# A graph layer and a routed expert layer on one core: the last tiles' list entries by one-hot products, the expert weights loaded in another order

## The reference

```python
x = x + gnn(layernorm(x), edges)                 # segment softmax over the edges of each row, then elu
x = x + ffn(layernorm(x))

def ffn(x):
    gate_logits = x @ gate_w + gate_b            # 16 experts
    topk_vals, topk_idx = jax.lax.top_k(gate_logits, 2)
    topk_w = jax.nn.softmax(topk_vals, axis=-1)
    h = jax.nn.relu(jnp.einsum('bsh,ehf->bsef', x, w1) + b1)        # 256 -> 512
    expert_out = jnp.einsum('bsef,efh->bseh', h, w2) + b2           # 512 -> 256
    y = x + jnp.sum(topk_w[..., None] * expert_out[topk_idx], axis=2)
    return layernorm(y) * gamma + beta
```

## Time and profile before

| | |
|---|---|
| time, median of 3 runs | 2786.66 us (2780.65 to 2787.5) |
| the profiled execution's own time | 2785.81 us |
| its span, first to last instruction | 2783.8 us |
| busy: PE, DVE, ACT, POOL | 1707.9, 1755.6, 1125.4, 1863.6 us |
| mean granted TensorE clock | 0.815 of full |
| HBM read and written | 355.94 and 36.52 MB |

### The profile page before, as it was taken

One profiled execution on the slowest core, in us unless ns is written; L12 is line 12 of the kernel. 1 busy time (PEld: TensorE's weight loads), 2 busy tenths in 40 slices (PEclk: granted clock), 3 DMA queues, 4 the chain that ended last, 5 costly groups with the idle time before them and its releaser, 6 DMA issues. The chain is left out here.

```text
span 2783.8 us, 44516 instructions
## 1 busy us (share of the span) xinstructions
PE 1707.9 (61%) x8882; PEld 1388.8 (50%) x8883; DVE 1755.6 (63%) x4256; ACT 1125.4 (40%) x2079; POOL 1863.6 (67%) x1938
## 2 busy tenths in 40 slices
PE   6445656556555556555566565655655638999970
PEld 5334444444444444444444444444444427999970
DVE  7655666666666566666666666666666636565557
ACT  3424344343443443443434434434344323443433
POOL 2267777777777777777777777777777624555543
PEclk9768877888888787788787787877877869999995
DMA  6445555555555555555555555555555355333346
GB/s 210 108 130 147 132 146 145 136 145 133 147 146 132 145 149 132 146 137 143 145 133 145 149 131 147 146 134 145 135 145 146 97 187 169 105 105 101 106 121 246
DMA packets 206790, 393.03 MB, mean 141 GB/s; under 512 B 73265, under 2 KB 129338, under 8 KB 200484
## 3 DMA queue, kind: packets, MB, share of 16 engines
q0 software_dynamic: 90992, 262.35, 36.9%
q1 hardware_dynamic: 93144, 109.62, 13.1%
q10 hardware_dynamic: 22620, 20.70, 2.6%
HBM read 355.94 MB, written 36.52 MB: 141 GB/s over the span
## 5 line engine op out<-in xcount | busy, mean ns | idle before, releaser
L1269 POOL DMA_INDIRECT gat<-table,idx x1627 | 1544.7, 949 | 505.4 <-issue 482.5
L1367 PE MATMUL ps_sum<-msg,hot 128*128 128x264 f32 x3322 | 1069.3, 492 | 778.8 <-DVE msg L1414 670.0
L1367 PEld LDWEIGHTS ps_sum<-msg,hot 128*128 128x128 f32 x3322 | 811.0, 250 | 985.1 <-issue 802.5
L1414 DVE TENSOR_TENSOR msg<-gat,ps_weight 128x2304 f32<-128x2304 f32 x196 | 471.6, 2406 | 31.1 <-ACT ps_weight L1324 27.3
L1324 ACT ACTIVATE ps_weight<-score 128x72 f32<-128x72 f32 x196 | 45.0, 230 | 591.1 <-DVE score L1405 590.9
L1411 DVE TENSOR_TENSOR hot<-ps_own,rel 128x1152 f32<-128x1152 f32 x196 | 250.3, 1277 | 0.0
L1403 DVE TENSOR_TENSOR both<-gat,ps_own 128x144 f32<-128x144 f32 x196 | 58.0, 296 | 288.0 <-DMA gat<-table,idx 286.7
L2116 PE MATMUL ps_ht<-xT,w_t 128*128 128x128 f32 x1712 | 214.7, 280 | 14.7 <-DVE w_t L2148 14.7
L2043 POOL DMA_INDIRECT chosen<-o_sb,put_at x105 | 115.6, 1101 | 148.2 <-DMA chosen<-o_sb,put_at 96.0
L2116 PEld LDWEIGHTS ps_ht<-xT,w_t 128*128 128x128 f32 x1712 | 205.4, 197 | 14.9 <-DVE w_t L2148 14.9
L2125 PE MATMUL ps_o<-w_sb,hidT 128*128 x840 | 200.0, 381 | 0.0
(11 more groups left out here) (397 smaller groups left out, 2124.5 us busy)
## 6 DMA issues: line engine op xcount, KB each, us to landing
dst_row<-dst_half SPq DMA_DIRECT2D x49, 1088.0 KB
gat<-table,idx POOLq DMA_INDIRECT x1661
b_t<-in_L_ffn_b_dram ACTq DMA_DIRECT2D x107, 128.0 KB, 3.0
w_sb<-in_L_ffn_w_dram SPq DMA_DIRECT2D x6, 2048.0 KB, 19.3
listing<-list_f SPq DMA_DIRECT2D x736, 0.5 KB
table<-rows SPq DMA_DIRECT2D x49, 128.0 KB, 1.7
y_rows<-y SPq DMA_DIRECT2D x49, 128.0 KB, 3.3
x_all<-in_x_dram SPq DMA_DIRECT2D x6, 896.0 KB, 8.9
```

Source lines behind the costliest of these rows:

```text
L1269: pool.indirect_dma_start(gat[:, GSTART[g] + k, :], None, table, bass.IndirectOffsetOnAxis(ap=idx[g][:, k:k + 1], axis=0)).then_inc(landed ...
L1367: made = pe.matmul(ps_sum[:, 0:SUM], hot[:, m, k, :], msg[:, m, k, :], start=(g == 0 and k == 0), stop=(g == NG - 1 and k == n - 1))
L1414: dve.tensor_tensor(msg[:, m, 0:n, 0:D].rearrange("p j (h d) -> p j h d", d=HD), gat[:, j:j + n, 0:D].rearrange("p j (h d) -> p j h d", d=HD),
```

## The change

- `settle` no longer computes addresses. For tiles 47 and 48 it keeps, for each expert, the place in its list (`late_place`); only tile 46 is scattered (two indirect writes in place of six), and the fetch of the lists waits for these two alone (`put` 32).
- The entries of tiles 47 and 48 come in by four products of one-hot matrices on PE (`late_row`, `late_lane`), accumulated in the bank where the fetched lists are transposed. DVE builds them while the fetch is under way.
- `y` of the last tile goes to another buffer (`xn`), and does not wait for the store of tile 47's.
- SP stores tile 47's `y` ahead of the first weights. The first load has three experts; the loads are 0-2, 3-4, 5-7, 8-11, 12-15. In the expert loop SP has at most two loads under way, and signals each one when it has landed, counting single experts.
- Four gathers of rows are issued ahead of the expert loop, in place of three.
- DVE's first 16 steps are written out (8 before). In steps 1 and on of these, gate and `minus_y` come before the copy of w1. The additions to `x_all` stand in steps 8 to 14.
- Four constants that POOL made with iota are derived by DVE from others.

```diff
-WLOADS = ((0, 2), (2, 4), (4, 8), (8, 12), (12, 16))
+DVE_HEAD = 4
+BETA_AT = 8
+WLOADS = ((0, 3), (3, 5), (5, 8), (8, 12), (12, 16))
...
-    def settle(self, dve, link, a, n, ps_route):
-        link(dve.tensor_tensor(self.base_f[:, :], self.base[:, :], self.expert_row[:, :], ALU.add))
+    def settle(self, dve, link, a, ps_route, place):
         dve.wait_ge(self.ranks_done, a + 1)
-        link(dve.tensor_tensor(self.base_f[:, :], self.base_f[:, :], ps_route[:, EXPERTS:2 * EXPERTS], ALU.add))
-        dve.tensor_tensor(self.base[:, :], self.base[:, :], ps_route[:, 2 * EXPERTS:3 * EXPERTS], ALU.add)
-        link(dve.tensor_tensor(self.hit[:, :, :], self.base_f[:, :].unsqueeze(1).to_broadcast([P, 2, EXPERTS]),
-                               self.pick[:, :, :], ALU.mult))
-        link(dve.tensor_reduce(self.at_f[:, :], self.hit[:, :, :], AX.X, ALU.add))
-        dve.tensor_copy(self.at_i[:, n, :], self.at_f[:, :]).then_inc(self.spots_ready, 1)
+        dve.tensor_tensor(place, self.base[:, :], ps_route[:, EXPERTS:2 * EXPERTS], ALU.add)
+        link(dve.tensor_tensor(self.base[:, :], self.base[:, :], ps_route[:, 2 * EXPERTS:3 * EXPERTS], ALU.add))
...
         @block.gpsimd
         def _(pool):
-            pool.iota(tile_of[:, :], pattern=[[0, 1]], base=0, channel_multiplier=1,
-                      allow_small_or_imprecise_dtypes=True).then_inc(consts, 1)
...
             pool.wait_ge(finish.listed, 16 * EXPERTS * (a - 1))
-            for n in range(3):
-                finish.scatter(pool, a - 1 + n, n)
+            finish.scatter(pool, a - 1)
             pool.wait_ge(steps, 1)
-            pool.wait_ge(finish.put, 96)
+            pool.wait_ge(finish.put, 32)
...
-            pool.wait_ge(steps, 4)
+            pool.wait_ge(steps, 5)
             pool.sem_inc(pool_turn, 1)
-            for i in range(FFN_AHEAD):
+            for i in range(FFN_BODY):
...
+            for c in range(4):
+                pe.matmul(ps_ids[:, 0:P], late_lane[:, c, :], late_row[:, c, :], start=(c == 0), stop=False)
+            pe.wait_ge(steps, 4)
+            pe.matmul(ps_ids[:, 0:P], ids_f[:, :], ident[:, :], start=False, stop=True).then_inc(turned, 1)
...
             sp.wait_ge(w_in[0], 32)
-            sp.sem_inc(w_ready, 1)
-            for k in range(FFN_AHEAD):
+            sp.sem_inc(w_ready, WLOADS[0][1])
+            for k in range(B):
                 sp.wait_ge(x_in[k], 16)
+            load_weights(sp, 1, w1, w2, w1_sb, w2_sb, w_in)
             for q in range(1, len(WLOADS)):
-                load_weights(sp, q, w1, w2, w1_sb, w2_sb, w_in)
-            for q in range(1, len(WLOADS)):
-                sp.wait_ge(w_in[q], 32)
-                sp.sem_inc(w_ready, (WLOADS[q][1] - WLOADS[q][0]) // 2)
+                if q + 1 < len(WLOADS):
+                    load_weights(sp, q + 1, w1, w2, w1_sb, w2_sb, w_in)
+                sp.wait_ge(w_in[q % 2], 32 * (q // 2 + 1))
+                sp.sem_inc(w_ready, WLOADS[q][1] - WLOADS[q][0])
...
-                if head and 1 <= i <= NGRP:
-                    if i == 1:
+                if head and 0 <= i - BETA_AT < NGRP:
+                    if i == BETA_AT:
                         dve.wait_ge(scale_in, 16)
```

More of the change, by code:

```diff
@@ L136, in build @@
         norms = Norms(sem)
-        w_in = [sem(f"w_in{q}") for q in range(len(WLOADS))]
+        w_in = [sem(f"w_in{q}") for q in range(2)]
         weights, listers, nodes = (ctx.enter_context(ExitStack()) for _ in range(3))
@@ L1706, in lower, with norm_outer @@
         act.activation(self.low[:, :], self.low[:, :], ACT.Exp).then_inc(self.exp_ready, 1)
-    def norm_outer(self, act, a):
+    def norm_outer(self, act, a, y=None):
         act.wait_ge(self.scale2_ready, a + 1)
-        if not (isinstance(a, int) and a == 0):
+        if y is None and not (isinstance(a, int) and a == 0):
             act.wait_ge(self.sent, a * 16)
-        act.activation(self.y[:, :], self.x(a), ACT.Identity, bias=self.nmr[:, bass.ds(a, 1)],
+        act.activation((self.y if y is None else y)[:, :], self.x(a), ACT.Identity, bias=self.nmr[:, bass.ds(a, 1)],
                        scale=self.rstd[:, bass.ds(a, 1)]).then_inc(self.y_ready, 1)
@@ L1935, in _ @@
             finish.weigh(dve, link, a, b)
+            dve.tensor_reduce(owner[:, :], mine[:, 1:X1], AX.X, ALU.add)
+            dve.scalar_tensor_tensor(held[:, :], tile_of[:, :].to_broadcast([P, 2]), -float(P), found[:, 1:3], ALU.mult, ALU.add)
+            link(dve.scalar_tensor_tensor(late_place[:, :, :], begin[:, 0:EXPERTS].unsqueeze(1).to_broadcast([P, 2, EXPERTS]), float(P),
+                                          late_place[:, :, :], ALU.mult, ALU.add))
+            dve.tensor_scalar(owner[:, :], owner[:, :], float(EXPERTS - 1), None, ALU.min).then_inc(steps, 1)
@@ new lines, in _ @@
+            dve.tensor_tensor(late_lane[:, :, :], late_lane[:, :, :],
+                              finish.ids[:, a:b + 1, :].rearrange("p t c -> p (t c)").unsqueeze(2).to_broadcast([P, 4, P]),
+                              ALU.mult).then_inc(steps, 1)
+            dve.wait_ge(ids_in, 16)
+            link(dve.scalar_tensor_tensor(ids_f[:, :], lane[:, :], held[:, 1:2], ids_f[:, :], ALU.is_lt, ALU.mult))
+            dve.tensor_tensor(ids_f[:, :], ids_f[:, :], rest[:, :], ALU.add).then_inc(steps, 1)
@@ L1936, in _ @@
+            dve.wait_ge(turned, 3)
+            link(dve.tensor_copy(put_all[:, :], ps_ids[:, 0:P]))
+            dve.tensor_scalar(get_all[:, :], put_all[:, :], 1, None, ALU.arith_shift_right).then_inc(steps, 1)
+            dve.wait_ge(steps, 5)
+            link(dve.scalar_tensor_tensor(second[:, :], get_all[:, :], -2.0, put_all[:, :], ALU.mult, ALU.add))
+            dve.tensor_copy(expert_l[0:1, 4:L + 4], ps_ids[0:1, P:2 * P])
             link(dve.tensor_scalar(passes_f[:, :], begin[:, EXPERTS:X1], float(FFN_LAG + FFN_BODY - 1), None, ALU.add))
@@ L2146, in first_weight, with weigh @@
                 e = expert(dve, i - back, -back)
-                dve.wait_ge(w_ready, (e >> 1) + 1)
+                dve.wait_ge(w_ready, e + 1)
                 dve.tensor_copy(w1_t[:, k % 2, :, :], one4(w1_sb[:, bass.ds(e, 1), :, :])).then_inc(w1_ready, 1)
+            def weigh(o, i, b):
+                dve.wait_ge(x_tr, i)
+                if not (isinstance(i, int) and i < 3):
+                    dve.wait_ge(o_ready, i - 2)
+                dve.scalar_tensor_tensor(gate[:, b:b + 1], xt[:, b, D + 1:YROW], second[:, bass.ds(i - 1, 1)], xt[:, b, D:D + 1],
+                                         ALU.mult, ALU.add)
+                dve.scalar_tensor_tensor(minus_y[:, o, :], xt[:, b, 0:D], second[:, bass.ds(i - 1, 1)], xt[:, b, 0:D],
+                                         ALU.mult, ALU.subtract).then_inc(gate_ready, 1)
             def step(k, i, head):
```

170 lines of the change are left out of this document (86 added, 84 removed).

## The result

| | before | changed |
|---|---|---|
| time, median, in the same session | 2785.76 us (2780.65 to 2787.5) | 2770.32 us (2768.5 to 2772.0) |
| the profiled execution's own time | 2785.81 us | 2769.94 us |
| its span | 2783.8 us | 2768.1 us |

The forecast was 2765 us, and the time lies in its range. 15.4 of the expected 21 us came. The ratios of the experiments leave out two executions, of 3595 and 6669 us, that ran at a lower granted clock than those beside them.

The account below looks back on a forecast made before the run. Bounds: a serial chain in the last tiles, DVE's wait for SP at loop start, then PE. First product -9.8 us; with the loop's deliveries tile 12 is -20.3, taken as -21: 2764.8, shown as 2765 us, range 2750 to 2776.

Parts of the forecast that it names:

- Last `y` in its own buffer, shorter `settle`: Last tiles: no wait for the earlier tile's store, -3.9 us; fewer small operations and no scatter for 47 and 48, -1.2.
- Lists without the last scatters: Last tiles: list fetch no longer waits for the last scatters; with the two parts before, gather -10.3 us, first product -9.8.
- The 3 MB load: First weight load, larger and later: landed by 2244, needed at 2255, so it costs nothing, with cover of 11 us.
- Signals load by load: Start of expert loop: DVE's 23.68 us wait for SP goes, and no copy waits again.
- What a tile costs beside a load: Expert loop while weights load: 6.66 us a delivery, from a single row, with bounds 3.76 and 8.3.
- x_all in steps 8 to 14: Expert loop: DVE's additions bound those steps at 4.51 us against 3.76; those beside the load are covered.
- behind tile 12 both programs are bound by PE: Rest of the expert loop: PE sets the pace in both programs, so the gain taken at tile 12, -21 us, stays.
- Stage 7: POOL's "ISA" instruction moves here: at 7.8 us it costs nothing, and idle time takes up to about 18 us.
- A: Expert loop: tiles lose nothing beside the load; tile 12 at about 2318, -36, 2750 us; chance 0.16.
- B: Expert loop: tiles lose more, 8.3 us a delivery; with dear one-hots 2774 us; chance 0.15 together with the late-signal rival.
- C: Expert loop: first copy waits if the 3 MB land after 2255; 2770 us at 2260; chance 0.15 with the dearer-tiles rival.
- D: Stage 7: moved instruction takes over 18 us and delays the additions; at 45 us, 2792 us; chance 0.03.

Follow-up runs that it names:

- the second profile: The changed kernel run and profiled once more, on a chip with 2791.93 us for the kernel before: 2773.89 us, ratio 0.9943.
- the run with the load ahead: The changed kernel with the first 3 MB load sent ahead of the store of tile 47's rows: 2774.68 us, ratio 0.9947.
- The run with the iota kept: The changed kernel with one POOL iota, whose result nobody reads, at the start of the last tiles: 2771.71 us.
- last tiles alone: The changed kernel with the old `stage6`, `load_weights` and `WLOADS`: ratio 0.9955.
- the old loads: The changed kernel with the old `WLOADS` (experts 0-1, 2-3, 4-7, 8-11, 12-15), signals still load by load: ratio 0.9947.
- without loads: The changed kernel with no weights issued in the expert loop, tiles from 4 on using expert 2's (another result): tile 40 at 170.3 us after the first product.
- the runs from step 3: The changed kernel with the `x_all` additions in steps 3 to 9: ratio 0.9951; the same with the first load ahead of tile 47's rows: 2766.63 us, ratio 0.9923.

## Why the prediction was right, and where it was off

The sum was -21 us. The traces have -16.2 from the mark to tile 40 (-16.0 in the second profile), and the medians -15.4 and -18.0. The gains came by the mechanisms told. What was missed is an overlap on PE, the landings beside the first load, and the end of the loop's slow part; each took from the gain.

- **Last `y` in its own buffer, shorter `settle`: right.** `xn_f` starts 0.04 us after its scale is written, and `row_i` comes 5.7 us sooner behind the mark (-5.1 forecast).
- **Lists without the last scatters: right in kind; the first product gained 7.5 us (8.8 in the second profile) where 9.8 was taken.** Behind the mark (2228.1 before), the forecast put the end of the one-hots at 20.9 us, the first gather at 23.6, the product at 28.9. The one-hots ended at 19.8, 1.1 sooner. Then the step that failed: "PE's product (0.5; its four others run meanwhile)". They read the last one-hot, so they run behind it, not meanwhile. In the run with the load ahead, where the lists were early, the gather left 4.1 us after the one-hots in place of the 2.7 reckoned: **1.4 us**. The products take 2.08 us at a granted clock of 0.50 (the lower level, 1.2 GHz), and part of that lies beside DVE's operations on `ids_f`. From gather to product it was 6.0 us where 5.3 was reckoned: 0.7.
- **The 3 MB load, "Nothing: cover of 11 us": right for its reader, wrong for its neighbours.** It was reckoned landed by 2244, at the full rate from its first byte, and landed at 2251.2; from 2239 to 2247 the core moved only 178 GB/s. Sending it ahead of tile 47's rows did not cure that (140 GB/s from 2243 to 2247). The run with the iota kept, in which they left later and the fall came later, points at tile 46's scatters of 4-byte elements; no run leaves them out, so the cause isn't shown. Nobody waited for the weights, but the fetch beside them took 5.0 us in place of 2.5, and the second scatter, reckoned landed, held it back by 0.6. That is the other 1.4 us of the first profile (0.2 in the second, with a landing of 4.5 and no wait for the scatter).
- **Signals load by load: right.** Without it 23.52 us are still waited (last tiles alone); with it none, or 3.30 with the old loads.
- **What a tile costs beside a load, 6.66 us: right,** though from a single row, and that it held so closely is in part luck. It was 6.73, and 3.93 without loads, where PE sets the pace. The Trainium skill ("DMA: Bandwidth & Descriptors", on arbitration) has each DMA engine take turns between queues, a packet at a time. The estimate drawn from that rule, that a delivery is held up by its own length, 0.4 us, isn't borne out here: the landing took 5.8 us beside the load and 3.5 without it.
- **x_all in steps 8 to 14: right in price; the end of its reach was missed.** Seven additions in the quiet cost 3.6 to 6.4 us over the same seven beside the loads (the runs from step 3), about the 7 x (4.53 - 3.76) that the step reckons with (its own row gives 4.51, not 4.53).
- **The loop at tile 40: 7.2 to 8.7 us in place of 11.2,** the larger part of the miss. From the first product to tile 12 the forecast has 76.9 us, and the profiles have 77.2 and 79.9: nearly nothing missed in the first, 3.0 us in the second. Then the step "behind tile 12 both programs are bound by PE": from tile 12 to tile 40 it was 104.6 us before and 106.1 and 105.0 in the changed kernel, 1.5 and 0.4 lost, and tiles 12 to 13 and 13 to 14 are still 4.85 and 4.19 us apart in the first profile. The last 0.7 is that -21 was taken where the deliveries gave -20.3. What the 3.0 us of the second profile are stays open.
- POOL's indirect writes beside an addition take longer: 2.35 us for tile 8's in the changed kernel, 2.70 without loads, 0.99 elsewhere. The Trainium skill ("SBUF — State Buffer", the rules on the shared port pair) has a DVE operation with two inputs in SBUF lock out a GpSimd operation that reads SBUF. The longer rows agree with that, though not every write beside an addition is long, and no run shows that it is the ports. Forecast to be free, it may be some of what the loop lacks; no run separates it.
- **Stage 7: right in what it costs.** The moved instruction takes up to 10.1 us there (from 2690.48, when the stage begins, to 2700.54), and beyond 9 us it moves the first addition, by 1.2 to 1.6 us. The end of the stage does not move.
- **The rivals.** A is out (6.73 us, not 3.8), B too (its own 8.3 us), C did not occur in this order, though its mechanism, a 3 MB load that is slower than its rate, is what stood beside the late lists; D's instruction stayed far from 18 us.
- **The signs.** Three of the prediction's own signs went against it, though the time came as forecast. DVE's second operation did wait for the fetch (2.38 us). The first product came at 2261.25, after the 2261 named as wrong; but the mark stood 1.9 us later in this execution, and behind it the product came at 31.2 us, where the limit was 32.9 and the forecast 28.9. And the first addition of stage 7 came 10.1 us into the stage, past the 9 us of rival D, of whose mechanism that much is there, at no cost. The 380 GB/s that are put down to the earlier trace rows aren't in them (355); single stretches of 4 us in the trace before have 380.

## What to carry to other kernels

A load that is early enough for its own reader may still be late for its neighbours: small transfers beside it land at twice their time, and in an order where a store stands behind it, the load's size comes straight into the chain (11.1 us in place of 4.3). Changes of loads and of what runs beside them should be tried together: with the old order of stores the third expert cost the loop's change 6 us, with the new it gained 2. An operand that is built in parts joins the chain with its last part, and so do all products of it. A small scattered write beside a bulk load may be dearer than it looks: here the load's rate fell from 391 to 132 GB/s behind two of them, which are a likely cause and not a shown one. Bulk loads that delay a serial chain of small landings were cheaper in a row than spread (one experiment, this loop), and other engines' extra work was cheapest beside them.

## What the runs showed of the hardware that was not expected

- Thirteen loads of 1 MB, one for every two tiles, cost 2.0 us each; in a row, 13 MB cost 1.0 to 1.1 us a megabyte.
- In two profiles the rate of a bulk load fell from 375 and 391 GB/s to 185 and 132, 5.8 and 7.5 us after two indirect writes of 4-byte elements were issued beside it, and those writes took 7.7 to 11.9 us to land. Which mechanism couples them isn't shown.
- POOL's instruction shown as "ISA", ahead of its first operation that is no indirect transfer, stands in up to 10.1 us of idle time in stage 7, for which the profile shows no other wait. It moves with the first such operation, so dropping four iotas does not drop it.
- One chip ran the same programs in 3428 us, 640 us more, all of it in the edge loop, where waits of POOL's gathers and of DVE were released by what the profile calls "remote", an event that it doesn't show. The stages behind were as long as on the other chips (`row_i` 15.4 to 15.5 us behind the mark on both). What it was stays open.
